# A gated linear recurrence: convolution and v x beta straight from PSUM, and a new order of work on every engine

## The reference, cut to what matters

```python
x = hidden_states                       # (4, 1024, 512), float32
xn = layernorm(x)
q, k, v = xn @ Wq, xn @ Wk, xn @ Wv     # 16 heads of 128
beta = sigmoid(xn @ Wb + bb)            # (B, L, H)
q = silu(causal_dwconv(q, qconv_w, qconv_b))      # 4 taps along the tokens
k = silu(causal_dwconv(k, kconv_w, kconv_b))
q, k = layernorm(q) * qn_w + qn_b, layernorm(k) * kn_w + kn_b   # per head
# per head, over the tokens t:
S = (1 - b_t) * S + b_t * outer(v_t, k_t)
o_t = S @ q_t
s = (o * silu(xn @ Wg)) @ Wo
# mixture of depths: the best half of the tokens of each sequence by a router score
g = silu(scatter(gelu(xn[idx] @ w1 + b1) @ w2 + b2))
out = x + s * g
```

## Time and profile before

| what | value |
| --- | --- |
| median of 3 runs (lowest, highest) | 2959.73 us (2956.99, 2960.72) |
| profiled execution, its span | 2957.1 us (the page gives no other time of it) |
| TensorE busy | 2656.4 us, 90% |
| VectorE busy | 2260.8 us, 76% |
| ScalarE busy | 1362.0 us, 46% |
| GpSimd busy | 1226.0 us, 41% |
| mean granted TensorE clock | 0.946 |
| first scatter of the recurrence, last | 142.6 us, 2113.5 us |

### The profile page before, as it was taken

How to read it: one execution, slowest core, us unless ns; L and a number is a source line. 1 busy time by engine, 2 the same in 40 slices (tenths; PEclk the granted TensorE clock), 3 DMA queues, 4 the chain that set the end, 5 groups by cost and what they waited for, 6 DMA issues and landing times. The chain is left out here.

```text
span 2957.1 us, 45164 instructions
## 1 busy us (share of the span) xinstructions
PE 2656.4 (90%) x15744; PEld 2319.3 (78%) x15744; DVE 2260.8 (76%) x3747; ACT 1362.0 (46%) x1777; POOL 1226.0 (41%) x517
## 2 busy tenths in 40 slices
PE   4789989999989989989999988999779999999997
PEld 4678878888878878878888877888668888788886
DVE  5699999999999999999999999999953121342332
ACT  5455555555555555545455455455433232332221
POOL 2155554555554556554546554555520000112221
PEclk8899999999999999999999999999889999999999
DMA  7222322332222243222224232222246110333320
GB/s 283 69 78 87 92 71 81 127 90 93 87 76 71 85 135 98 81 84 71 85 78 142 85 92 71 85 78 78 72 153 221 43 57 28 107 121 100 99 85 28
DMA packets 257402, 278.85 MB, mean 94 GB/s; under 512 B 55494, under 2 KB 211398, under 8 KB 252618
## 3 DMA queue, kind: packets, MB, share of 16 engines
q1 hardware_dynamic: 162506, 143.97, 15.7%
q10 hardware_dynamic: 86144, 109.06, 11.4%
q0 software_dynamic: 8704, 25.19, 2.7%
HBM read 214.70 MB, written 71.86 MB: 97 GB/s over the span
## 5 line engine op out<-in xcount | busy, mean ns | idle before, releaser
L880 DVE SCALAR_TENSOR_TENSOR xn_rows<-raw,rc_conv,xn_rows 128x1024 f32<-128x1024 f32 x384 | 625.8, 1637 | 22.9 <-ACT xn_rows L778 13.7
L1042 PE MATMUL rc_ps_proj<-xt_hi,w_hi 128*128 128x512 f32 x1024 | 453.1, 442 | 78.8 <-ACT rc_v_raw L802 60.4
L697 POOL TENSOR_TENSOR rc_small<-rc_small,rc_minus_half 128x16 f32<-128x16 f32 x64 | 244.7, 3824 | 545.8 <-DVE rc_small L909 545.8
L1044 PE MATMUL rc_ps_proj<-xt_hi,w_lo 128*128 128x512 f32 x1024 | 426.6, 417 | 0.0
L1043 PE MATMUL rc_ps_proj<-xt_lo,w_hi 128*128 128x512 f32 x1024 | 426.3, 416 | 0.0
L837 ACT ACTIVATE rc_tok_k<-rc_tok_k,rc_small 128x128 f32<-128x128 f32 x512 | 204.3, 482 | 447.1 <-DVE rc_small L914 447.1
L1042 PEld LDWEIGHTS rc_ps_proj<-xt_hi,w_hi 128*128 128x128 f32 x1024 | 208.8, 204 | 127.2 <-ACT rc_v_raw L802 69.4
L1061 PE MATMUL rc_ps_proj<-wv_hi,xt_hi 128*128 128x256 f32 x1024 | 294.7, 288 | 0.0
L1062 PE MATMUL rc_ps_proj<-wv_lo,xt_hi 128*128 128x256 f32 x1024 | 289.4, 283 | 0.0
L1063 PE MATMUL rc_ps_proj<-wv_hi,xt_lo 128*128 128x256 f32 x1024 | 289.3, 282 | 0.0
L683 POOL TENSOR_TENSOR rc_k_state<-rc_tok_k,rc_k_norm_rows 128x1024 f32<-128x1024 f32 x64 | 204.2, 3190 | 107.8 <-ACT rc_tok_k L837 107.7
(11 more groups left out here) (174 smaller groups left out, 6693.2 us busy)
## 6 DMA issues: line engine op xcount, KB each, us to landing
rc_decay_all<-scratch_decay ACTq DMA_DIRECT2D x64, 512.0 KB, 4.0
rc_cum_all<-scratch_cum ACTq DMA_DIRECT2D x64, 512.0 KB, 4.7
scratch_o<-rc_o_sb ACTq DMA_DIRECT2D x64, 512.0 KB, 3.2
w_raw<-in_wq SPq DMA_DIRECT2D x64, 256.0 KB, 3.2
w_raw<-in_wk SPq DMA_DIRECT2D x64, 256.0 KB, 3.5
wv_raw<-in_wv SPq DMA_DIRECT2D x32, 512.0 KB, 4.9
rc_score_all<-scratch_score SPq DMA_DIRECT2D x32, 512.0 KB, 4.0
raw<-in_w SPq DMA_DIRECT2D x16, 512.0 KB, 3.5
```

The costliest lines, as they stand in the source:

```text
L697: nc.gpsimd.tensor_tensor(small[:, 6], small[:, 5], minus_half[:], ALU.pow).then_inc(S["rstd_done"], 1)
L880: nc.vector.scalar_tensor_tensor(out=act_cm[j], in0=raw[j][:, t:t + L], scalar=conv[B_.par][:, j, t:t + 1], in1=act_cm[j], op0=ALU.mult, o ...
L1042: nc.tensor.matmul(out, hi, xt_hi[:, k, cols], start=k == 0, stop=False)
L1044: last = nc.tensor.matmul(out, lo, xt_hi[:, k, cols], start=False, stop=k == KC - 1)
```

## The change

DVE reads the projections of q and k out of PSUM for the convolution, and the projection of V for v x beta, so that the copies `raw` and `v_raw` go. The convolution moves from B to A, the step of its projection, and PE's next projection into the slot waits for the last tap. v x beta is computed for both heads of a pair, half of the tokens in each step, one step after the projection; `v_beta` holds two heads and two pairs, and the loop body holds two pairs (four steps), so that the buffer is known at build time. The order in every queue is new:

The core of the diff:

```diff
-            with eng.Fori(PEELED_PAIRS, PAIRS - 1) as u:
-                for par in range(2):
-                    step(u, par)
-            for i in range(N - 2, N + LAG_D):
-                step(i // 2, i % 2)
+            with eng.Fori(PEELED_PAIRS, PAIRS - 2, 2) as u:
+                for odd in range(2):
+                    for par in range(2):
+                        step(u + odd, par, odd)
+            for i in range(N - 4, N + LAG_D):
+                step(i // 2, i % 2, i // 2 % 2)
...
-                sp.wait_ge(S["q_conv"], PAD * N)
-                sp.wait_ge(S["k_conv"], PAD * N)
...
-                def own_raw(j):
+                def tap(j):
 
                     n = "qk"[j]
                     after_step(act, n + "_projected", A_.i)
-                    after_step(act, n + "_conv", A_.i - 1, PAD)
-                    nc.scalar.activation(raw[j][:, PAD:], proj_of(j), ACT.Copy).then_inc(S[n + "_raw"], 1)
...
                 def convolve(j):
 
                     n = "qk"[j]
-                    after_step(dve, n + "_raw", B_.i)
-                    after_step(dve, n + "_tap", B_.i)
+                    projected = ps_proj[:, (par + j) % 2]
+                    after_step(dve, n + "_tap", A_.i)
                     for t in range(PAD):
+                        back = PAD - t
                         if t:
-                            after_step(dve, n + "_conv", B_.i, PAD, t)
-                        nc.vector.scalar_tensor_tensor(out=act_cm[j], in0=raw[j][:, t:t + L],
-                                                       scalar=conv[B_.par][:, j, t:t + 1], in1=act_cm[j],
+                            after_step(dve, n + "_conv", A_.i, PAD, t)
+                        nc.vector.scalar_tensor_tensor(out=act_cm[j][:, back:], in0=projected[:, 0:L - back],
+                                                       scalar=conv[par][:, j, t:t + 1], in1=act_cm[j][:, back:],
                                                        op0=ALU.mult, op1=ALU.add).then_inc(S[n + "_conv"], 1)
...
-                    after_step(dve, "v_copied", 2 * C_.pair + 1)
-                    after_step(dve, "outputs_mm", C_.i - 2)
-                    after_step(dve, "updates_mm", C_.i - 2)
-                    gate = keep["beta_steps"][:, :, bass.ds(C_.i, 1)].to_broadcast([P, NC, P])
-                    nc.vector.tensor_tensor(v_beta[C_.par][:], v_raw[:, :, C_.par], gate, ALU.mult
+                    after_step(dve, "v_projected", B_.i)
+                    after_step(dve, "outputs_mm", 2 * B_.pair - 3)
+                    first = B_.par * VC
+                    gate = keep["beta_steps"][:, first:first + VC, bass.ds(B_.pair * 2, 2)].unsqueeze(3)
+                    nc.vector.tensor_tensor(v_beta[B_.pair_par][:, first:first + VC],
+                                            ps_proj[:, B_.par].rearrange("p (c h t) -> p c h t", h=2, t=P),
+                                            gate.to_broadcast([P, VC, 2, P]), ALU.mult
                                             ).then_inc(S["v_beta_done"], 1)
...
                     if half == 0 and pos == 0:
                         after_step(pe, "w_hi_done", A_.i)
                         after_step(pe, "w_lo_done", A_.i)
-                        after_step(pe, "k_tap", A_.i - 1)
+                        after_step(pe, "k_conv", A_.i - 1, PAD)
                     elif half == 0:
-                        after_step(pe, "v_copied", A_.i - 1)
+                        after_step(pe, "v_beta_done", A_.i - 1)
...
                         after_step(pe, "wv_lo_done", A_.pair)
-                        after_step(pe, "q_tap", A_.i)
+                        after_step(pe, "q_conv", A_.i, PAD)
...
                 if B_.live:
                     after_step(pe, "q_silu", B_.i)
-                    after_step(pe, "q_ready", C_.i)
-                    turn(work(par, 2), lambda c: act_cm[0][:, c * P:(c + 1) * P]).then_inc(S["q_turned"], 1)
+                    after_step(pe, "outputs_done", D_.i - 1)
+                    turn(work(par, QT), lambda c: act_cm[0][:, c * P:(c + 1) * P]).then_inc(S["q_turned"], 1)
```

More of the change, by code:

```diff
@@ L750, in load_cum, with step @@
                               ).then_inc(cum_loaded[par], 16)
-            def step(u, par):
-                A_, B_, C_, D_, nxt = (At(u, par, lag) for lag in (0, LAG_B, LAG_C, LAG_D, -1))
+            def step(u, par, odd):
+                A_, B_, C_, D_, nxt = (At(u, par, lag, odd) for lag in (0, LAG_B, LAG_C, LAG_D, -1))
                 proj_of = lambda pos: ps_proj[:, (par + pos) % 2]
@@ L831, in step @@
                     nc.scalar.activation(w_hi[nxt.par][:], w_raw[nxt.par][:], ACT.Copy).then_inc(S["w_hi_done"], 1)
+                if C_.live:
+                    ready(1, "k_back", "k_ready", k_cm[C_.par])
+                    load_cum(C_.par, C_.i, C_.pair)
+                if B_.live:
+                    tokens(1)
+                if A_.live:
+                    tap(1)
                 if B_.live:
@@ L970, in step @@
                     after_pair(dve, cum_loaded[D_.par], D_.pair)
-                    updates = chunks(work(par, 5))
+                    updates = chunks(work(par, UP))
                     nc.vector.tensor_copy(states[:, 0], updates[:, 0]).then_inc(S["states_done"], 1)
@@ L1019, in turn, with step @@
                 return last
-            def step(u, par):
-                A_, B_, C_, D_ = (At(u, par, lag) for lag in (0, LAG_B, LAG_C, LAG_D))
+            def step(u, par, odd):
+                A_, B_, C_, D_ = (At(u, par, lag, odd) for lag in (0, LAG_B, LAG_C, LAG_D))
                 def project(pos, half):
@@ L1089, in step @@
                 if D_.live:
+                    after_step(pe, "k_state_done", D_.i)
+                    after_step(pe, "v_beta_done", 2 * D_.pair + 1)
+                    if C_.live:
+                        after_step(pe, "k_ready", C_.i)
+                    else:
+                        after_step(pe, "scores_done", D_.i - 1)
+                    for c in range(NC - 1):
+                        last = nc.tensor.matmul(work(par, UP)[:, c * P:(c + 1) * P], k_state[D_.par][:, c],
+                                                v_beta[D_.pair_par][:, c, D_.par], start=True, stop=True)
@@ L1098, in step @@
                     for c in range(NC):
                         t = slice(c * P, (c + 1) * P)
-                        last = nc.tensor.matmul(work(par, 4)[:, t], k_cm[D_.par][:, t], q_cm[D_.par][:, t],
+                        last = nc.tensor.matmul(work(par, SC)[:, t], k_cm[D_.par][:, t], q_cm[D_.par][:, t],
                                                 start=True, stop=True)
@@ L1128, in step @@
                     for c in range(NC):
-                        out = work(par, 6)[:, c * P:(c + 1) * P]
-                        last = nc.tensor.matmul(out, scores[:, c], v_beta[D_.par][:, c], start=True, stop=c == 0)
+                        out = work(par, OUT)[:, c * P:(c + 1) * P]
+                        values = v_beta[D_.pair_par][:, c, D_.par]
+                        last = nc.tensor.matmul(out, scores[:, c], values, start=True, stop=c == 0)
                         if c:
```

180 lines of the change are left out of this document (73 added, 107 removed).

## The result

The changed kernel takes 2820.11 us (median of 4 runs, 2817.73 to 2824.76); the kernel before, measured beside it, 2958.36 (4 runs, 2956.81 to 2960.72). The ratio is 0.9531, 95% interval [0.9519, 0.9544]. The prediction was 2829, range 2745 to 2905. The profiled execution of after took 2817.73 us, its span is 2815.9.

A forecast was written before the change was run, and what follows sets the result against it. VectorE, bound by SBUF contention with GpSimd, would drop below TensorE's 27.7 us a step, GpSimd's run holding even steps. 2957.1 - 122 (31 pairs, 3.95 each) - 8 (ends) = 2827 span, so 2829 us; range 2745 to 2905.

The forecast's parts named there:

- the layout: Recurrence laid out step by step: even 31.3 us, odd 28.35, pair 59.65 against 63.6; likeliest 2829 us, chance 0.44.
- Taps, v x beta, shift: On VectorE: six taps some 2.1 us less a step, v x beta 2.2 less, shift 2.1 less; together 6.4 us.
- The wait for wv_lo: Even step, before V: TensorE ready at 18.9, waits until 20.8 for wv_lo, a new stall of 1.9 us.
- The held variance: Even step: VectorE's variance blocked by GpSimd's wv_lo and add to 23.2 us, done 23.7; the step takes 31.3.
- rival (a): Even step: variance slips between GpSimd's instructions, TensorE sets the step at 30.3 us; pair 58.65, 2799 at least; chance 0.27.
- The wait for silu(q): Both steps: TensorE waits about 0.7 us at the transposes of silu(q).
- rival (b): Even step: TensorE's clock falls behind the gap before V, costing 2.4 us a pair, 2903 in all; chance 0.09.
- Rival (c): Loop bodies of four steps don't stay resident; 14 jumps back cost 29 to 87 us, 2858 to 2916; chance 0.11.
- All engines pausing once in four steps: Sign, at the jump back of the four-step loop body, that would show the prediction wrong; no size given.
- The ends: Outside the pairs: start-up 6 us less, drain about 4 less, loads of x 2 more; together 8 less.
- The load of the next sequence's x: On SP: second half of x starts after V as before but is needed 0.8 us sooner, three times; 2 more.
- The read of PSUM: Skill page: 120 fixed cycles from PSUM, 58 from SBUF, 12 us over the kernel; the prediction followed rows showing no difference.

The follow-up runs named there:

- experiment 2: Changed kernel with GpSimd's power ahead of the add for k (first kernel, 2770.85 us), or wv_lo and power ahead of q_cum and the add (second, 2683.45 us).
- Experiments 3 and 4: 3: changed kernel, taps from SBUF copies, 2905.09 us, with q_cum late too 2953.7; 4: kernel before, w_hi earlier, w_lo ahead of power, 2957.17 us.
- experiment 1: Changed kernel with wv_lo ahead of w_lo and q_cum on GpSimd in the even step, nothing else: 2803.02 us, ratio 0.9473.
- the first kernel of experiment 2: Changed kernel with power ahead of the add for k on GpSimd, q_cum still ahead of wv_lo: 2770.85 us, ratio 0.9363.
- the best kernel: Changed kernel with GpSimd's even-step order k_weighted, w_lo, wv_lo, power, q_cum, add for k: 2683.45 us, ratio 0.9068.
- its two variants: Kernel before with w_hi earlier on ScalarE and w_lo ahead of power on GpSimd, 2957.17 us; kernel before with four-step loop bodies, 2981.79 us.
- the reordered kernel of before: Kernel before with w_hi ahead of the copy of k on ScalarE and w_lo ahead of power on GpSimd: 2957.17 us, ratio 0.9989.

## Why the prediction was right, by its own steps

- **What bounds.** The sum was right: VectorE under TensorE, and the steps set by how the two and GpSimd interlock. Odd step 27.89 us against 28.35 laid out; even step 31.08 against 31.3; a pair 58.97 against 59.65. TensorE's own work was laid out as 27.7 us; experiment 2 shows 27.13 to 27.24. Its wait in the layout, 7.3 - 6.5, is 0.8 and was carried on as 0.7.
- **Taps, v x beta, shift.** 1.28, 1.22 and 0.17 us against 1.28, 1.2 and 0.2. Experiments 3 and 4 show that it is the second SBUF operand that waits, and not the read of PSUM that is quick.
- **The wait for wv_lo.** 1.9 us expected, 49.5 / 26 = 1.9 measured, at most 2.2. But it doesn't set the step, as experiment 1 shows.
- **The held variance.** Expected until 23.2 in the step, three GpSimd instructions in a row. The trace shows one small sum let through for each; rival (a), that they slip between, is refuted for after. In the odd step the layout had the scan held to 9.0 and VectorE at the variance when GpSimd was done. The trace shows the scan 0.14 us ahead of k_weighted and not held; it is k_weighted that takes 4.33 us:

```profile
1003.86 2.28 DVE L924 TENSOR_TENSOR_SCAN rc_dmat<-rc_decay_all,rc_chunk_ident 128x1024 f32<-128x1024 f32 x1
```

```profile
1004.00 4.33 POOL L672 TENSOR_TENSOR rc_k_state<-rc_tok_k,rc_k_norm_rows 128x1024 f32<-128x1024 f32 x1 [9.13 <-ACT rc_tok_k L821]
```

VectorE is at the variance 1.4 us sooner than laid out and L886 is held 1.4 us, until GpSimd's add ends, at 19.8 in the step as laid out (19.9). So the odd step came out right by GpSimd's end, past a scan that was read wrongly.
- **The wait for silu(q).** 0.7 us a step expected, 24.6 / 55 = 0.45 measured. It vanishes when VectorE is in time (experiment 2).
- **The clock.** 0.98 on average, as laid out, but rival (b) came in part: behind 12 of the 26 waits for wv_lo, of 1.86 us and no longer than the rest, TensorE ran 3.3 us of V at half clock about 1 us after its start, and V took 7.5 us and not 6.0 (rows below). The even step is 31.08 (31.47 at a jump back) with and without it: without, the outputs wait 0.6 us for the scores, with it they don't, so the held variance hides the fall. It was priced at 2.4 us a pair and cost nothing here; that it cost nothing is luck of this order, as the first kernel of experiment 2 shows, where it costs 1.5. Where the load of xt_lo held TensorE, the clock stayed full behind 2.78 us and fell for some 3.4 us behind 2.93 and 3.40.
- **Code fetches.** Rival (c) was right in its mechanism and wrong in its price for this kernel: 88 packets, and VectorE's 13 pauses, 23.6 us in the window (the row of L913 above). Ten of the pauses last 1.05 to 1.3 us and the three at changes of sequence 3.9 to 4.1. They go into the wait for tap(q) that VectorE has later in the same step: it is 2.94 us in plain even steps and 0.8 where the loop jumps back. What reaches the step is 31.47 - 31.08 = 0.4 us, mostly ScalarE's. All engines pausing once in four steps was given as a sign that the prediction is wrong; VectorE and ScalarE pause, TensorE does not.
- **The ends.** The mis-sized term. The load of the next sequence's x was put at 2 us more for all three; the three steps took 2.7, 4.4 and 4.8 us over 31.08, 11.8 in all. The first had no fall of the clock; the other two had, and are 1.7 and 2.1 us longer with load waits 0.15 and 0.62 longer, so the clock makes about 1.5 of each (an estimate), 3 of the 11.8, and the jump back 0.4 of each. Others cover it: the pairs gained 34.54 + 29.08 - 58.97 = 4.65 us each and not 3.95 (31 x 0.7 = 22 more), the jumps outside those steps took 10 x 0.4 = 4, the sequences 10 more than priced. Together that is 8 better than the layout, and the span came out at 2815.9 against 2827; the other 3 are the ten even steps of the kernel before that took 29.35 and not 29.08. The start and the drain gave the 10 us that they were priced at. That the forecast lies within 9 us is partly luck: 25 us of errors one way and 14 the other cancel.
- **The read of PSUM.** The Trainium skill ("VectorE: DVE Perf Modes", "The TRN2 errata") would have had every changed instruction cost more from PSUM, by 12 us in all. No trace here shows it: 1218 ns for the scores with one operand in PSUM against 1216 for k_state with both in SBUF, both 128x1024 f32 and undisturbed; a tap takes 1.28 us from either memory.
- **What fits the fetches.** The Trainium skill ("Runtime: NRT & Kernel Launch", "Instruction fetch mechanics") says that a taken branch to code outside the resident window stalls the engine. VectorE agrees (20 packets with two steps in the body, 88 or 89 with four). TensorE, to which the Trainium skill gives a larger store in the same section, shows no pause at the jump.

Busy time by stretches (the granted clock is the third number from the end), kernel after: V in an even step without a fall, the slow stretch of V in the next even step, and a change of sequence just after TensorE's start at 1033.41 and in its slow stretch.

```profile
930.10:936.10 6.00, 5.97 (x48) 5.81 (x48) 5.65 (x13) 0.00 (x0) 5.08 (x2) 1.00 0.27 87
990.10:993.40 3.30, 3.30 (x18) 3.30 (x17) 3.10 (x10) 0.00 (x0) 2.66 (x2) 0.50 0.47 155
1033.41:1034.40 0.99, 0.99 (x4) 0.86 (x5) 0.00 (x0) 0.66 (x1) 0.91 (x1) 1.00 0.94 194
1034.40:1037.80 3.40, 3.40 (x9) 2.52 (x9) 2.99 (x2) 0.40 (x1) 0.00 (x0) 0.51 1.04 302
```

What stays open: what an earlier load of xt_lo would give at the changes of sequence (not tried), why the clock falls behind some waits of 1.86 us and not behind others, what the first kernel of experiment 2 would take without its falls, and whether a VectorE body short enough to stay would bring the best kernel below 2683.

## What to carry to other kernels

When two engines hold each other up, look at where each instruction reads, not only at how long it is: here a VectorE instruction with one operand in PSUM kept its time beside GpSimd (a tap 1.28 us), and one with two SBUF operands that met a running GpSimd instruction waited until that one ended, even on 16 elements. Then place the second engine's run beside the first one's PSUM instructions; source and order were worth little apart (7 us for the best order with the taps from SBUF, 85 for the taps in the order of after, 277 for both together), so try them together; the source in the order of before was not tried. And before an observed wait is taken for the cause, ask what would be late at the next meeting point were it gone: here removing TensorE's largest wait gave 17 us, shortening VectorE's hold, which no view of TensorE named, gave 49 with that wait kept, and removing both gave 137.

## What the runs showed of the hardware that was not expected

- The contention goes both ways. GpSimd's power took 3.84 us in the kernel before and 2.92 in after, on the same 16 elements. Before, it started 0.16 us behind k_state on VectorE (two SBUF operands, 1026.66 to 1027.88), and its 3.84 is 2.92 and about the rest of that instruction. It takes 3.84 in all three kernels in which k_state stands right ahead of it (before and its two variants) and 2.92 in all seven with the new order; an edit that moves k_state alone was not run. Likewise k_weighted takes 2.35 us alone and 4.33 where the scan came first.
- A VectorE instruction with one SBUF tensor and scalars may be held too: the comparison of the ranks (L974) has a mean of 1.51 us in after, where the same one took 0.75 before (753 ns also in the reordered kernel of before). In after it lies beside k_weighted, before beside nothing of GpSimd's; the instruction ahead of it (L970), also with one SBUF tensor, keeps its 1.25 us beside the same k_weighted. No run isolates this.
- The small sums are let through one for each GpSimd instruction, at its end, also when GpSimd has its next one queued without a gap (1052.28 in the timeline above).
- A jump back in a loop costs ScalarE 1.0 us (27 times, with no packets for it), and VectorE, with a fetch, 0.9 to 1.6 us, or 3.8 to 4.7 where it falls on a change of sequence. That the load of the next sequence, at the same time, delays the fetch is only argued.
- TensorE's clock can fall unseen: the mean of 0.98 in the window of after covers 12 falls to half clock behind waits of 1.86 us, and no step is longer for them.
